# An embedding tower on one core: lookups and pair products taken in turns on TensorE

## The chip, the cores and the metric

The kernel runs on one core of one Trainium2 chip. The metric is the device time of one execution in microseconds (us); the kernel before has a median of 606.28 us in three runs (603.73 to 606.65). Engines are named as in the profile: PE is TensorE (PEld its weight loads), DVE is VectorE, ACT is ScalarE, POOL is GpSimd, SP is SyncE.

## The reference

For 2048 samples, 27 table rows of 128 numbers each are looked up, all pairs of the 27 are multiplied, and the 351 products go with a dense input through three layers.

```python
e = jnp.stack([tbl_f[ids[:, f]] for f in range(27)], axis=1)        # 2048 x 27 x 128
interactions = jnp.einsum('bfd,bgd->bfg', e, e)
x = interactions.reshape(B, F * F)[:, TRIL_IDX]                      # 351 pairs
z = jnp.concatenate([bottom_mlp_out, x], axis=1)
h = jnp.concatenate([z, bottom_mlp_out], axis=1)
h = jnp.maximum(h @ W_top1 + b_top1, 0.0)                            # 512
h = jnp.maximum(h @ W_top2 + b_top2, 0.0)                            # 256
y = h @ W_top3                                                       # 2048 x 1
```

Tables have 1000 to 125000 rows. Everything is float32.

## The kernel before

The 2048 samples are cut into 16 halves of 128 (h = 0 to 15). Features come in two ways.

Nine small tables ("hot", k = 0 to 8) are kept in SBUF as `parts` (a high and a low part, f32r). They are looked up by matmul: VectorE makes masks (`mask[...] = (hot_i == rowid)`, 1 where a sample's id is the row), and PE multiplies chunks of 125 table rows with a mask. One lookup serves a window of four halves (512 columns), and each half does the share of one part of the window: a **pair** of tables (8 chunks, in each chunk 2 tables x 2 parts = 4 matmuls, 32 in all; in the profile 32 records), and in h = 0, 4, 8, 12 a **single** table besides (10 chunks, 20 matmuls). `AFTER[h]` names them, `look_up` is PE's side, `make_masks` and `copy_lookup` those of VectorE and ScalarE. There are 8 mask buffers; a mask of the next lookup is made when a chunk of the present one has retired (`masks_used`). The copies go to `eH` and ScalarE places them in `eT` (`place_early`, `place_late`).

The other 18 tables are gathered by POOL, 18 indirect DMAs a half (L284), into `rows[:, h % 2]`. PE transposes them (L664, 18 matmuls in five groups) into PSUM banks, VectorE and ScalarE copy them to `eT`. The gathers for h + 2 may start when PE has transposed the rows of h; POOL waits for it group by group (L280 to L288).

The products of a half, the "gram", are 64 matmuls of 58 x 52 columns (L681), two records each in the profile since they are fp32, so 128 records. They go in 4 sets of 32 records over three PSUM banks (`gram_bank`): a set is copied by VectorE (strip 0, L582) and ScalarE (strip 1, L424) into `pairs`, and the fourth set needs the bank of the first. When all four are copied, SP moves `pairs` to `x` (L322). Every two halves form a tile of 256 samples for the layers (`layer1` L700 and L704, `layer2` L736, `layer3` L744), which PE takes in pieces after the gram and between the transposes.

Each engine's stream is written out by hand; semaphores order them against each other. In the loop over h = 1 to 14, PE takes: transposes (with pieces of the layers between), the pair's lookup, the whole gram, the single lookup, layers. VectorE takes: copies of transposes, all masks it may make, the lookup's copy, then the gram's copies (`copy_pairs`). For h = 0 the gram comes first and the pair's lookup after it.

## Time and profile before

| | |
|---|---|
| median of three runs | 606.28 us (603.73 to 606.65) |
| the profiled execution | 607.63 us, its span 605.8 us |
| mean granted clock of PE | 0.806 |
| PE busy | 415.0 us (69%), 3512 matmul records |
| PEld busy | 347.6 us (57%) |
| POOL busy | 300.4 us (50%) |
| DVE busy | 216.8 us (36%) |
| ACT busy | 150.6 us (25%) |
| chain that ended last | PE 57%, "issue" 27%, ACT 4%, DVE 2%, DMA 2% |

The table is from the profile's first page. A busy share is an average over the span. "issue" is time in which an engine waited for nothing that the profile shows. The start of a PE record is when it was begun, but its end is modelled, so when PE's work was really done is read from the engines that waited for it.

### The profile page before, as it was taken

The numbers are of one execution on the slowest core, as the hardware profiler recorded it, in microseconds if no ns is written. First come the engines' busy times: TensorE is split into PE (matmuls) and PEld (weight loads), VectorE is DVE, ScalarE is ACT, GpSimd is POOL, SyncE is SP. The second block draws the span as 40 slices with busy tenths as digits, with TensorE's granted clock in tenths as the row PEclk, the third lists the DMA queues.
The fourth block names the chain that finished last, engine by engine and source line by source line (L and its number), as shares of the span: only waits on it lengthen the run. The fifth ranks groups of instructions, "written<-read, shape, count | busy, mean of one in ns | idle before, by whom it ended". The sixth has DMA issues, their size and how long they took to land.

```text
span 605.8 us, 8753 instructions
## 1 busy us (share of the span) xinstructions
PE 415.0 (69%) x3512; PEld 347.6 (57%) x3512; DVE 216.8 (36%) x396; ACT 150.6 (25%) x333; POOL 300.4 (50%) x295
## 2 busy tenths in 40 slices
PE   2941586874876739768494857959586573946997
PEld 2941475663765638556383736837475562835886
DVE  4842448424251334514223245423313232312230
ACT  3320232030422113121130503213031311403533
POOL 6777623757273741737447271574717364271000
PEclk9966688877895959959597887968779695966999
DMA  8764203112121311113121130212102131120000
GB/s 222 211 202 113 56 23 109 50 49 90 27 79 36 112 35 53 49 34 93 36 75 48 37 107 24 66 51 81 48 30 72 28 94 36 32 52 22 27 8 14
DMA packets 20450, 39.81 MB, mean 66 GB/s; under 512 B 7167, under 2 KB 11475, under 8 KB 20410
## 3 DMA queue, kind: packets, MB, share of 16 engines
q0 software_dynamic: 9312, 18.94, 12.1%
q1 hardware_dynamic: 11036, 20.25, 11.6%
q8 instruction: 28, 0.46, 0.3%
q14 instruction: 12, 0.10, 0.1%
q10 hardware_dynamic: 62, 0.06, 0.0%
HBM read 36.14 MB, written 0.01 MB: 60 GB/s over the span
## 4 chain that ended last, share of the span: by engine, by line
PE 57%; issue 27%; another core or an unknown queue 6%; ACT 4%; DVE 2%; DMA 2%; SPq 1%; ACTq 0%; DVEq 0%
PE gram_bank L681 20%; PE col_bank L650 20%; PE mlp_bank L704 5%; PE mlp_bank L736 5%; PE col_bank L664 2%; PE mlp_bank L700 2%; DMA pairs<-in_tbl 2%; DVE mask L547 1%; ACT eT L389 1%; PE mlp_bank L744 1%; ACT h L440 1%; DVE eT L572 1%; ACT eT L394 1%; ACT parts L372 1%
## 5 line engine op out<-in xcount | busy, mean ns | idle before, releaser
L284 POOL DMA_INDIRECT rows<-in_tbl,idx x288 | 298.6, 1037 | 249.2 <-PE col_bank L664 160.1
L681 PE MATMUL gram_bank<-eT 128*58 128x52 f32 x2048 | 123.4, 261 | 136.7 <-issue 135.2
L681 PEld LDWEIGHTS gram_bank<-eT 128*58 128x58 f32 x2048 | 102.6, 174 | 160.2 <-issue 160.0
L650 PE MATMUL col_bank<-mask,parts 125*128 125x512 f32 (+3 forms) x708 | 157.8, 386 | 18.3 <-DVE mask L547 11.7
L650 PEld LDWEIGHTS col_bank<-mask,parts 125*128 125x128 f32 x708 | 131.7, 209 | 40.5 <-DVE parts L588 11.7
L547 DVE TENSOR_SCALAR mask<-hot_i,rowid 125x1024 fp32r<-125x1024 int32 (+3 forms) x152 | 103.2, 679 | 117.3 <-remote 62.3
L582 DVE COPY pairs<-gram_bank 26x208 f32<-26x208 f32 x128 | 46.7, 365 | 120.0 <-remote 100.0
L424 ACT ACTIVATE pairs<-gram_bank 26x208 f32<-26x208 f32 x128 | 44.0, 344 | 139.8 <-remote 114.1
L381 ACT ACTIVATE eH<-col_bank 128x512 f32<-128x512 f32 (+3 forms) x26 | 13.0, 506 | 226.0 <-remote 150.9
L664 PE MATMUL col_bank<-ident,rows 128*128 128x128 f32 x288 | 41.0, 287 | 31.6 <-ACT eH L381 18.9
L664 PEld LDWEIGHTS col_bank<-ident,rows 128*128 128x128 f32 x288 | 34.8, 148 | 38.1 <-issue 35.6
L572 DVE COPY eT<-col_bank 128x512 f32<-128x512 f32 (+1 forms) x38 | 24.4, 653 | 88.8 <-PE col_bank L664 75.2
L704 PE MATMUL mlp_bank<-x,w 126*128 126x256 f32 (+3 forms) x192 | 44.8, 369 | 0.0
L394 ACT ACTIVATE eT<-eH 128x256 f32<-128x256 f32 (+1 forms) x64 | 36.5, 703 | 10.2 <-DVE eH L564 9.8
L704 PEld LDWEIGHTS mlp_bank<-x,w 126*128 126x128 f32 (+1 forms) x192 | 35.4, 193 | 4.9
L389 ACT ACTIVATE eT<-col_bank 128x512 f32<-128x512 f32 (+1 forms) x42 | 26.0, 629 | 35.2 <-PE col_bank L664 21.0
L736 PE MATMUL mlp_bank<-h,w 128*128 128x256 f32 (+1 forms) x128 | 31.1, 400 | 0.2 <-ACT h L433 0.2
L551 DVE TENSOR_SCALAR mask<-hot_i,rowid 125x512 fp32r<-125x512 int32 (+2 forms) x50 | 20.2, 451 | 25.3 <-DMA hot_i<-in_hot_ids 11.0
L736 PEld LDWEIGHTS mlp_bank<-h,w 128*128 128x128 f32 x128 | 24.7, 208 | 4.2 <-ACT h L433 0.4
L292 POOL DMA_DIRECT2D x<-pairs x3 | 1.6, 533 | 41.2 <-DVE pairs L582 41.2
L700 PE MATMUL mlp_bank<-bottom,w 128*128 128x256 f32 (+1 forms) x64 | 19.8, 391 | 1.2 <-ACT y L449 1.2
L588 DVE TENSOR_TENSOR parts<-pairs,parts 125x1024 fp32r<-125x1024 f32 (+1 forms) x9 | 11.1, 1261 | 14.0 <-ACT parts L372 7.7
(31 smaller groups left out, 82.0 us busy)
## 6 DMA issues: line engine op xcount, KB each, us to landing
hot_i<-in_hot_ids SPq DMA_DIRECT2D x13, 512.0 KB
rows<-in_tbl,idx POOLq DMA_INDIRECT x288
pairs<-in_tbl SPq DMA_DIRECT2D x8, 448.0 KB
hot_i<-in_hot_ids SPq DMA_DIRECT2D x5, 256.0 KB
bottom<-in_bottom SPq DMA_DIRECT2D x8, 128.0 KB
hot_i<-in_hot_ids SPq DMA_DIRECT2D x2, 384.0 KB
x<-pairs SPq DMA_DIRECT2D x16, 39.0 KB
pairs<-in_tbl SPq DMA_DIRECT2D x1, 560.0 KB
```

Of the source, the lines that this page charges most:

```text
L284: pool.indirect_dma_start(out=rows_of(h, g)[:, i * D:(i + 1) * D], out_offset=None, in_=tables[GATHERED_TABLES[f]], in_offset=bass.Indirec ...
L389: nc.scalar.activation(out, src, ACT.Copy).then_inc(col_copied[fill % BANKS], 1)
L394: return nc.scalar.activation(eT[:, :, first:last].rearrange("p s f -> p f s"), eH[:, first:last, at:at + HALF], ACT.Copy)
L424: last = nc.scalar.activation(pairs_of(s, 1, j), gram_of(n % BANKS, 1, j), ACT.Copy)
L547: last = nc.vector.tensor_scalar(mask[0:ROWS, entry % MASKS, 0:2 * size], ids, row_of(ks[0], c), None, ALU.is_equal)
L582: last = nc.vector.tensor_copy(pairs_of(s, 0, j), gram_of(n % BANKS, 0, j))
L650: last = nc.tensor.matmul(col_bank[fill % BANKS][:, 0:size], parts[k][0:ROWS, part, c * D:(c + 1) * D], mask[0:ROWS, entry % MASKS, at:at ...
L664: last = nc.tensor.transpose(col_bank[fill % BANKS][:, i * HALF:(i + 1) * HALF], rows_of(h, g)[:, i * D:(i + 1) * D], ident[:, :])
L681: last = nc.tensor.matmul(gram_bank[n % BANKS][COLUMNS * t:COLUMNS * t + GRAM_ROWS, q, 0:PACK * (F - 1)], eT[:, a:a + PACK, :].rearrange(" ...
L700: nc.tensor.matmul(layer1_out(u, m), w1[:, X_CHUNKS, m * 128:(m + 1) * 128], bottom[:, buf, at:at + size], start=True, stop=False)
L704: last = nc.tensor.matmul(layer1_out(u, m).rearrange("p (h s) -> p h s", s=HALF), w1[0:k, c, m * 128:(m + 1) * 128], x[0:k, buf, at // HAL ...
L736: last = nc.tensor.matmul(layer2_out(u, m), w2[:, c, m * 128:(m + 1) * 128], h1[:, c, at:at + size], start=(c == 0), stop=(c == N1 // 128 ...
```

## The change

On PE, `look_up_and_multiply` takes a half's pair of lookups in eight turns: one chunk (4 matmuls), then half a gram set (8 matmuls, 16 records). The wait for the features to be placed (`features_placed`) stands after the first chunk. This holds for h = 0 to 14, h = 0 too, where the gram had come first. The single lookup and the last half stay as they were. On VectorE, `masks_and_pairs` makes two of the eight masks ahead of each set's copy, and copies the lookup after the four sets; before, all masks and the lookup's copy came ahead of the four. On ScalarE the gram's copies now come ahead of the lookup's copy.

```diff
@@ ScalarE, the loop over h @@
+                copy_pairs(h)
                 if h < LAST:
                     copy_lookup(AFTER[h][0])
-                copy_pairs(h)
-                if h < LAST:
                     place_early(h + 1)
@@ VectorE @@
+            def masks_and_pairs(h):
+                single = AFTER[h][1:]
+                ahead = AFTER[h + 1][:1] if h + 1 < LAST else []
+                early = ENTRIES[single[0]] if single else 0
+                each = MASKS // SETS
                 for s in range(SETS):
+                    for entry in range(s * each, (s + 1) * each):
+                        if entry < early:
+                            make_masks(single[0], slice(entry, entry + 1))
+                        elif ahead:
+                            make_masks(ahead[0], slice(entry - early, entry - early + 1))
+                    copy_set(h, s)
+                copy_lookup(AFTER[h][0])
+                if early and ahead:
+                    make_masks(ahead[0], slice(MASKS - early, MASKS))
+                for n in single:
+                    copy_lookup(n)
...
@@ PE @@
+            def look_up_and_multiply(n, h):
+                parts_of_set = TURNS // SETS
+                chunks, steps = CHUNKS[LOOKUPS[n][0][0]] // TURNS, STRIP // PACK // parts_of_set
+                for turn in range(TURNS):
+                    look_up(n, slice(turn * chunks, (turn + 1) * chunks))
+                    if turn == 0:
+                        features_placed(h)
+                    at = turn % parts_of_set * steps
+                    multiply_set(h, turn // parts_of_set, slice(at, at + steps))
...
-            multiply_pairs(0)
-            for n in AFTER[0]:
+            look_up_and_multiply(AFTER[0][0], 0)
+            for n in AFTER[0][1:]:
                 look_up(n)
...
-                look_up(AFTER[h][0])
-                multiply_pairs(h)
+                look_up_and_multiply(AFTER[h][0], h)
                 for n in AFTER[h][1:]:
                     look_up(n)
```

On PE in a half like h = 2, before: the last transposes (L664), the pair's lookup (L650), the gram (L681), `layer1` (L700, L704).

```order
L664 MATMUL col_bank<-ident,rows 128x128 x18
L650 MATMUL col_bank<-mask,parts 128x512 x32
L681 MATMUL gram_bank<-eT 58x52 x64
L700 MATMUL mlp_bank<-bottom,w 128x256
L704 MATMUL mlp_bank<-x,w 128x256 x3
```

The same place on PE after the change (L665 transposes, L651 lookup, L683 gram); the pattern of two rows goes on until there are eight of each.

```order
L665 MATMUL col_bank<-ident,rows 128x128 x18
L651 MATMUL col_bank<-mask,parts 128x512 x4
L683 MATMUL gram_bank<-eT 58x52 x8
L651 MATMUL col_bank<-mask,parts 128x512 x4
L683 MATMUL gram_bank<-eT 58x52 x8
L651 MATMUL col_bank<-mask,parts 128x512 x4
L683 MATMUL gram_bank<-eT 58x52 x8
```

The 32 lookup matmuls and 64 gram matmuls stand in eight alternating groups of 4 and 8; their numbers are the same.

On VectorE in a half like h = 6, before: copies of transposes (L572), masks (L547), the lookup's copy (L564), the gram's copies (L582).

```order
L572 COPY eT<-col_bank 128x128x4
L572 COPY eT<-col_bank 128x128x3
L547 TENSOR_SCALAR mask<-hot_i,rowid 125x1024 x8
L564 COPY eH<-col_bank 128x512
L582 COPY pairs<-gram_bank 26x26x8 x8
```

And after the change (L573, L548, L582, L565).

```order
L573 COPY eT<-col_bank 128x128x4
L573 COPY eT<-col_bank 128x128x3
L548 TENSOR_SCALAR mask<-hot_i,rowid 125x1024 x2
L582 COPY pairs<-gram_bank 26x26x8 x2
L548 TENSOR_SCALAR mask<-hot_i,rowid 125x1024 x2
L582 COPY pairs<-gram_bank 26x26x8 x2
L548 TENSOR_SCALAR mask<-hot_i,rowid 125x1024 x2
L582 COPY pairs<-gram_bank 26x26x8 x2
L548 TENSOR_SCALAR mask<-hot_i,rowid 125x1024 x2
L582 COPY pairs<-gram_bank 26x26x8 x2
L565 COPY eH<-col_bank 128x512
```

Each set's two copies now stand behind two masks, and the lookup's copy behind the last set.

## Rows read from the trace of the kernel before

**Rows 1.** The page's groups: busy, mean ns of one | idle before, its releaser

```profile
L284 POOL DMA_INDIRECT rows<-in_tbl,idx x288 | 298.6, 1037 | 249.2 <-PE col_bank L664 160.1
L681 PE MATMUL gram_bank<-eT 128*58 128x52 f32 x2048 | 123.4, 261 | 136.7 <-issue 135.2
```

**Rows 2.** Timeline, h = 6, PE: start us, us, engine, line, records [idle before]

```profile
276.07 7.54 PE L650 MATMUL col_bank<-mask,parts 125*128 125x512 f32 x32 [0.37 <-issue]
283.54 0.79 PE L681 MATMUL gram_bank<-eT 128*58 128x52 f32 x21
284.65 0.32 PE L681 MATMUL gram_bank<-eT 128*58 128x52 f32 x4 [0.33 <-issue]
...
298.92 4.24 PE L681 MATMUL gram_bank<-eT 128*58 128x52 f32 x78 [0.46 <-issue]
```

**Rows 3.** Timeline, POOL: first and last of 18 gathers, and the next first

```profile
273.21 0.94 POOL L284 DMA_INDIRECT rows<-in_tbl,idx  x1 [9.45 <-PE col_bank L664]
...
295.71 0.94 POOL L284 DMA_INDIRECT rows<-in_tbl,idx  x1 [0.30 <-issue]
309.62 0.94 POOL L284 DMA_INDIRECT rows<-in_tbl,idx  x1 [12.97 <-PE col_bank L664]
```

**Rows 4.** Timeline, h = 6, VectorE: masks, the lookup's copy, the gram's copies

```profile
279.46 3.30 DVE L547 TENSOR_SCALAR mask<-hot_i,rowid 125x1024 fp32r<-125x1024 int32 x4 [3.50 <-DMA hot_i<-in_hot_ids]
283.25 0.85 DVE L547 TENSOR_SCALAR mask<-hot_i,rowid 125x1024 fp32r<-125x1024 int32 x1 [0.48 <-PE col_bank L650]
284.69 0.75 DVE L547 TENSOR_SCALAR mask<-hot_i,rowid 125x1024 fp32r<-125x1024 int32 x1 [0.59 <-remote]
...
287.59 0.75 DVE L547 TENSOR_SCALAR mask<-hot_i,rowid 125x1024 fp32r<-125x1024 int32 x1 [0.69 <-issue]
288.50 0.69 DVE L564 COPY eH<-col_bank 128x512 f32<-128x512 f32 x1 [0.16 <-issue]
299.13 1.61 DVE L582 COPY pairs<-gram_bank 26x208 f32<-26x208 f32 x4 [9.93 <-remote]
```

**Rows 5.** Timeline, PE: the last gram burst of h = 2, 3, 4, 9

```profile
154.83 3.48 PE L681 MATMUL gram_bank<-eT 128*58 128x52 f32 x83 [0.28 <-issue]
...
190.52 2.23 PE L681 MATMUL gram_bank<-eT 128*58 128x52 f32 x38 [0.47 <-issue]
...
223.69 5.34 PE L681 MATMUL gram_bank<-eT 128*58 128x52 f32 x105 [0.46 <-issue]
...
410.13 0.67 PE L681 MATMUL gram_bank<-eT 128*58 128x52 f32 x9 [0.98 <-issue]
```

**Rows 6.** DMA queues, SP's packets, 198.1 to 222.6 (h = 4), 383.8 to 410.3

```profile
q1 hardware_dynamic: 529, 1.00, 14.3%
...
q1 hardware_dynamic: 8, 0.01, 0.1%
```

**Rows 7.** Timeline: two masks of h = 1, each after a chunk; gram in h = 9

```profile
107.32 0.75 DVE L547 TENSOR_SCALAR mask<-hot_i,rowid 125x1024 fp32r<-125x1024 int32 x1 [2.39 <-PE col_bank L650]
108.96 0.76 DVE L547 TENSOR_SCALAR mask<-hot_i,rowid 125x1024 fp32r<-125x1024 int32 x1 [0.88 <-PE col_bank L650]
...
394.62 2.33 PE L681 MATMUL gram_bank<-eT 128*58 128x52 f32 x79
```

**Rows 8.** Timeline, h = 0, PE: the gram, then lookups of the pair and the single

```profile
79.50 1.40 PE L681 MATMUL gram_bank<-eT 128*58 128x52 f32 x45 [1.54 <-ACT eT L394]
...
85.94 12.09 PE L650 MATMUL col_bank<-mask,parts 125*128 125x512 f32 x52
```

**Rows 9.** Windows: length, PE, PEld, DVE, ACT, POOL busy (x), PEclk, DMA share, GB/s

```profile
298.90:303.00 4.10, 4.08 (x78) 4.07 (x78) 2.19 (x6) 2.04 (x6) 0.00 (x0) 0.50 0.00 0
...
303.10:309.00 5.90, 5.90 (x28) 5.13 (x28) 0.73 (x2) 3.64 (x8) 0.00 (x0) 0.94 0.09 24
...
281.00:286.80 5.80, 3.96 (x40) 3.04 (x39) 3.83 (x6) 0.00 (x0) 4.58 (x5) 1.00 0.17 45
286.80:298.90 12.10, 3.38 (x22) 2.27 (x21) 1.55 (x3) 0.60 (x1) 7.72 (x8) 0.50 0.20 50
```

More of the change, by code:

```diff
@@ L31 @@
 SLOTS = 2
+TURNS = 8
 STAGES = 3
@@ L478, in _ @@
             copy_pairs(0)
+            copy_lookup(AFTER[0][0])
             place_early(1)
-            for n in AFTER[0]:
+            for n in AFTER[0][1:]:
                 copy_lookup(n)
@@ L594, in _ @@
                 make_masks(n)
[L596 to L601 removed]
+            make_masks(AFTER[0][0])
+            masks_and_pairs(0)
             dve.wait_ge(weights_loaded, 16 * WEIGHT_LOADS)
             nc.vector.tensor_tensor(w1[:, X_CHUNKS, :], w1[:, X_CHUNKS, :], wb, ALU.add).then_inc(w1_summed, 1)
[L604 to L607 removed]
             for h in range(1, HALVES):
@@ L610, in _ @@
                     copy_transposed(h, g)
-                if h == LAST:
-                    copy_pairs(h)
-                elif len(AFTER[h]) == 2:
-                    pair, single = AFTER[h]
-                    make_masks(single)
-                    make_masks(AFTER[h + 1][0], slice(0, free))
-                    copy_lookup(pair)
-                    copy_pairs(h)
-                    make_masks(AFTER[h + 1][0], slice(free, MASKS))
-                    copy_lookup(single)
-                else:
-                    if h + 1 < LAST:
-                        make_masks(AFTER[h + 1][0])
-                    copy_lookup(AFTER[h][0])
-                    copy_pairs(h)
+                if h < LAST:
+                    masks_and_pairs(h)
+                else:
+                    for s in range(SETS):
+                        copy_set(h, s)
         @block.tensor
@@ L632, in fill_free, with look_up @@
                     pe.wait_ge(col_copied[fill % BANKS], fill // BANKS)
-            def look_up(n):
+            def look_up(n, part=slice(None)):
                 ks, _, wide = LOOKUPS[n]
                 size, chunks = wide * HALF, CHUNKS[ks[0]]
-                for k in ks:
+                for k in ks if range(chunks)[part][0] == 0 else ():
                     fill_free(lookup_fill(n, k))
@@ L641, in look_up @@
                         pe.wait_ge(low_made, k + 1)
-                for c in range(chunks):
+                for c in range(chunks)[part]:
                     entry = entries_to(n) + c * len(ks) // 2
@@ L755, in _ @@
             pe.wait_ge(pads_cleared, 1)
-            multiply_pairs(0)
-            for n in AFTER[0]:
+            look_up_and_multiply(AFTER[0][0], 0)
+            for n in AFTER[0][1:]:
                 look_up(n)
@@ L785, in _ @@
             transpose(LAST, 4)
-            multiply_pairs(LAST)
+            features_placed(LAST)
+            for s in range(SETS):
+                multiply_set(LAST, s)
             layer3(TILES - 2)
```

50 lines of the change are left out of this document (21 added, 29 removed).

## Prediction

> **What bounds the kernel now.** Three views, in this order. First the page's groups: 288 gathers on POOL and 2048 gram matmul records on PE; before the gram records PE stands idle for 136.7 us, all but 1.5 us of it charged to "issue", that is to nothing the profile can name [rows 1]. Second, PE's timeline of one half, h = 6 [rows 2]: the pair of lookups is recorded smoothly, 32 records in 7.54 us, then 21 gram records in a burst, then three or four at a time with gaps, until at 298.92 the remaining 78 go through in 4.24 us. Third, who else moves then. POOL issues its 18 gathers from 273.21 to 296.65 [rows 3], and PE is free again 2.3 us after the last one. The next 18 start at 309.62, after the gram, the MLP and the next transposes, because POOL waits for PE's transposes. So a half is a loop: gathers (some 23.5 us), 2.3 us, then what PE still has to do, then transposes, then gathers again. Only what PE does **after the gathers** lies on the path; what it does beside them is free.
>
> How fast PE really is beside the gathers is read from its waiters, since ends of matmuls are modelled. VectorE makes a mask each time a chunk (4 lookup records) retires: one wait ends at 284.69, the next but one at 287.59, so 1.45 us a chunk or 0.36 us a record, where they were recorded at 0.236 us [rows 2, 4]. The first gram set (32 records) retires when VectorE copies it at 299.13: (299.13 - 287.59) / 32 = 0.36 us a record again [rows 4]. A record with 512 columns and one with 52 cost the same. Beside the gathers PE therefore seems limited by the **number of instructions**, not by their work. In PE's timeline the records run some 32 ahead of what has retired (the first set was recorded complete at about 288).
>
> How many of a half's 160 records (32 lookups, 128 gram) are out when PE is freed differs: the last burst has 83, 38, 105 and 9 gram records in h = 2, 3, 4 and 9 [rows 5]. Over h = 2 to 12, h = 4, 8, 12 are like the 105, four like the 83, three like the 38, one like the 9; h = 1 is like the 38 and h = 13 like the 105 with lookups half as wide. The half with 105 had 529 packets of SP's queue beside its gathers, the one with 9 had 8 [rows 6], which again looks like a shared allowance of events.
>
> **The change, part by part.** The number of instructions on PE is the same. What moves is their order: 8 turns of 4 lookup records and 16 gram records instead of 32 and then 128. If the allowance counts instructions, a half gets as many records past the gathers as before, but what is **left over** is no longer all gram: a fifth of it is lookups.
>
> Prices. At full clock a lookup record takes 0.236 us [rows 2] and a gram record 0.031 (45 in 1.40 us [rows 8]); a turn 4 x 0.236 + 16 x 0.031 = 1.44 us. At half clock a chunk takes 108.96 - 107.32 = 1.64 us, 0.41 a record [rows 7], and a gram record 4.24 / 78 = 0.054 [rows 2]; a turn 2.5 us. The clock is 0.50 from 286.8 to 303 and 0.94 after it [rows 9], so I take the first 4.5 us after the gathers at half clock (1.8 turns), the rest at full.
> - Like 105: 55 records past, 5.25 turns left: 4.5 + 3.45 x 1.44 = 9.5 us for 5.3 now [rows 5]: +4.2, three times 12.6; h = 13 about +2.
> - Like 83 or 78: 3.9 to 4.15 turns left: 7.5 to 7.9 us for 4.2 and 3.5: +3.9, four times 15.6.
> - Like 38: 1.9 turns left: 4.6 for 2.2: +2.4, four times 9.6.
> - Like 9: 0.45 turn: +0.4.
>
> Together **+40 us**, if the same count gets past. That is one end. The other end: in the stretch before PE slows down, PE is limited by its work (a chunk of 8 instructions in 0.94 us), and a turn of 40 instructions in 1.44 us would get 19 more a us through, if slowing sets in by the clock on the wall and not by a count. In h = 6 that stretch is some 4 us (the first mask that waits late is at 283.25, before it the chunks were in time): 1.9 turns gained. In the halves like 105 I take 2 us (1 turn), in those like 38 the whole lookup. Gained: 3 x 1.4 for the first kind, 4 x 2.8, 4 x 4.6, 1.1 and 1.4: **-36 us**. Nothing in the trace settles which end holds. For a count: in h = 9 PE was never slowed in the lookups and then slowed right after 79 gram records in 2.33 us [rows 7]. For the clock on the wall: at 79 records the count was far higher than in h = 6. I take half, -18.
>
> Front, h = 0: the gram waits for ScalarE until 79.50 and runs to 85.94, 6.4 us for 128 records that take 4.0 at full clock, then the pair of lookups [rows 8]. Interleaved, the first chunk can go under that wait and most turns run at full clock: -2 us, between 0 and -4.
>
> VectorE: two masks now stand ahead of each set's copy. Behind them on VectorE wait the copy, and behind that PE's fourth set (turn 7), which needs the first set's bank. The masks wait for SP's transfer of ids; in h = 6 the first four start at 279.46 and take 3.30 us [rows 4]. Two masks then end by 281.1, the copy by 281.9, and PE reaches turn 7 at 276.07 + 6 x 1.44 = 284.7 at the earliest. Nothing, with 2.8 us to spare; without that cover it would cost what the ids are late. The sets' copies by VectorE and ScalarE now fall beside the gathers, but the last set's does not, and a copy from a lookup's bank comes after it on each (VectorE's takes 0.69 us [rows 4]): under the 5 to 6 us of MLP that PE runs next, so nothing, except in h = 1, which has no MLP there (at most 1.5 us). The new wait for the last features stands after the first chunk instead of after eight; they are copied within half a us of its start, under 0.94 us of chunk. POOL and SP keep their order; nothing is moved past their queues.
>
> Sum: 607.63 (the profiled execution; its span is 605.8, 1.8 us lie around it) + 40 - 18 - 2 = 627.6. That execution is 1.35 us above the median of the runs, so **626 us** on the median's scale.
>
> A rule that speaks for the change: the clock follows how densely PE works, and PE falls to 0.50 in the thin gram phase at 286.8 [rows 9]. The Trainium skill, "TensorE: Matmul & The Clock Gate", section "HAM oscillation — how this bites in real kernels", has it that gaps in PE's work throw it back to the low clock, so that work placed into the gaps should hold it up. By it this case would come out as the third rival below; the rows so far only show that the clock held while slowed lookups ran (281 to 286.8, 1.00) and fell in thin gram.
>
> **The rivals.**
> 1. A pure count. +40 - 2: 644; with all leftover turns at half clock (5.25 x 2.5 for 9.5, and so on, +60) 664. For it: 0.36 us a record for both kinds. Against it: the counts in h = 6 and 9 differ threefold.
> 2. Slowing by the clock on the wall. 607.6 + 40 - 36 - 2 - 1.35 = 608. For it: POOL's pace is constant.
> 3. The clock stays up. All leftover turns at 1.44 us: +2.3, +1.7, +0.5 for the three kinds, +17 in all with h = 13, less half of what is gained before slowing (14) and the front's 2: 608. Against it: at 0.36 us a record a turn of 1.44 us of work takes 7.2 us.
> 4. The other side: the gaps belong to runs of gram matmuls. "Issue" stands ahead of gram and hardly ahead of lookups [rows 1, 2]; four lookups between would cover the gaps, PE would be done with its 160 records (11.6 us) long before the gathers end, and the last bursts (44 us over h = 1 to 13, from 5.34 down to 0.67 [rows 5]) would leave the path: 563. It decides if a chunk of lookups beside gathers retires at its own pace; in h = 6 it did not [rows 4].
> That the change does not do what it says is excluded by the order: PE's stream is in program order.
>
> **How the numbers follow.** Chances: my forecast (612 to 640) 0.35, pure count 0.17, by the wall 0.13, clock up 0.12, gaps covered 0.18, other losses 0.05 (VectorE's copies late after all). A measurement of this kernel tells about 0.5% from no change, 603.2 to 609.3: of the wall and clock cases 0.14 lie in it and 0.05 below. So faster 0.23, same 0.14, slower 0.63. The range takes in the wall case and the pure count with part of its cold end, and leaves out the covered gaps and the far end: 599 to 650.
>
> **What would show it.** In the profile after, PE's timeline of a half should show thin records of both lines beside the gathers, a last burst that holds lookups, longer than 4.2 us (7 us in halves like h = 6), and gathers that start some 2 us later in each period. A half whose gram is over before the gathers end, or a period near 25 us, would prove rival 4. If the waits charged to "issue" keep their sum but the burst is short, the wall case holds. A granted clock of 1.00 beside the gathers would be rival 3.

## The result, and the profile after

The changed kernel takes **677.51 us** (median of 4 runs, 675.77 to 679.25) where the kernel before, timed beside it, takes 606.25 (603.73 to 606.65): ratio 1.1185, 95% interval 1.1143 to 1.1228. A later pair of timings gave 675.94 against 603.92, ratio 1.1199 (1.1134 to 1.1263). The prediction said slower, 626 us, at most 650. The direction was right, and so was the place, the work after the gathers; the loss is 71 us instead of 20.

The profiled execution has a span of 675.2 us, 69.4 more than before. The page's groups of the changed kernel, as [rows 1]:

```profile
L285 POOL DMA_INDIRECT rows<-in_tbl,idx x288 | 283.6, 985 | 329.0 <-PE col_bank L665 238.9
L651 PE MATMUL col_bank<-mask,parts 125*128 125x512 f32 (+3 forms) x708 | 216.4, 441 | 47.1 <-issue 27.4
L683 PE MATMUL gram_bank<-eT 128*58 128x52 f32 x2048 | 127.3, 242 | 144.5 <-issue 144.0
```

Gram matmuls are as busy as before (127 against 123 us) and idle time charged to "issue" now stands ahead of the lookups too. A gather is shorter (985 ns instead of 1037), but POOL waits 239 us for PE's transposes instead of 160: the whole loss and more in one number, 79 us, of which shorter gathers give a part back. PE's timeline of h = 6, as [rows 2] (start us, length, line, records, idle before):

```profile
296.36 1.17 PE L651 MATMUL col_bank<-mask,parts 125*128 125x512 f32 x4 [0.37 <-issue]
297.45 0.64 PE L683 MATMUL gram_bank<-eT 128*58 128x52 f32 x16
...
316.57 0.32 PE L683 MATMUL gram_bank<-eT 128*58 128x52 f32 x1 [1.17 <-issue]
317.96 2.62 PE L651 MATMUL col_bank<-mask,parts 125*128 125x512 f32 x4 [1.06 <-issue]
320.51 1.04 PE L683 MATMUL gram_bank<-eT 128*58 128x52 f32 x16
321.48 2.08 PE L651 MATMUL col_bank<-mask,parts 125*128 125x512 f32 x4
323.49 1.04 PE L683 MATMUL gram_bank<-eT 128*58 128x52 f32 x16
324.46 1.39 PE L651 MATMUL col_bank<-mask,parts 125*128 125x512 f32 x4
325.78 0.64 PE L683 MATMUL gram_bank<-eT 128*58 128x52 f32 x16
326.35 1.19 PE L651 MATMUL col_bank<-mask,parts 125*128 125x512 f32 x4
...
329.74 0.48 PE L714 MATMUL mlp_bank<-bottom,w 128*128 128x256 f32 x1
```

The last of this half's 18 gathers ends at 316.35. Two turns get past in a burst, then PE is thin (20 records from 301.0 to 317.2, windows below; the third turn among them), and behind the gathers stand **five** turns of lookups and gram, 11.8 us, where the kernel before had 78 gram records in 4.24 us [rows 2]. The last burst holds lookups, as predicted. A turn takes 3.5 and 3.0 us first, then 1.9 and 1.7. VectorE in the same half, as [rows 4]:

```profile
301.37 0.75 DVE L548 TENSOR_SCALAR mask<-hot_i,rowid 125x1024 fp32r<-125x1024 int32 x1 [5.12 <-issue]
311.04 0.75 DVE L548 TENSOR_SCALAR mask<-hot_i,rowid 125x1024 fp32r<-125x1024 int32 x1 [8.91 <-remote]
319.51 0.74 DVE L582 COPY pairs<-gram_bank 26x208 f32<-26x208 f32 x2 [7.72 <-remote]
```

Two masks stand beside the gathers, where there were eight at 279.46 to 288.34 [rows 4]: the other six now wait behind the first set's copy, and that waits for the thin gram. The windows, as [rows 9] (length, busy time and count of PE, PEld, DVE, ACT, POOL, granted clock, DMA share, GB/s):

```profile
301.00:317.20 16.20, 4.81 (x20) 2.64 (x20) 1.51 (x2) 0.00 (x0) 12.00 (x12) 0.61 0.21 54
...
318.00:323.40 5.40, 5.17 (x24) 2.79 (x23) 2.87 (x6) 1.38 (x4) 0.00 (x0) 0.50 0.01 3
323.40:330.00 6.60, 6.60 (x78) 4.88 (x78) 3.64 (x6) 0.85 (x3) 0.00 (x0) 0.89 0.00 0
```

**The account.** Cut both traces at the ends of the gathers, h = 1 to 13, and the 69.4 us come out in five parts. "Past" is how many of a half's pair lookups and gram matmuls (160 records) have their start by 1.9 us after the last gather, mean of h = 2 to 12; "work after" is from the last gather's end to the start of the last of these 160, summed over h = 1 to 13 (negative where all 160 start before the gathers end); "rest" is from there to the next gather, and "tail" what follows the last of h = 13. The other rows are experiments told below.

| | past | start of h = 1 | gathers | work after | rest | tail | span |
|---|---|---|---|---|---|---|---|
| before | 92 | 98.7 | 307.2 | 70.5 | 79.9 | 49.4 | 605.8 |
| changed | 64 | 93.6 | 292.7 | 163.0 | 74.6 | 51.3 | 675.2 |
| PE's order undone | 65 | 92.4 | 295.0 | 95.9 | 74.9 | 49.8 | 608.0 |
| before, masks twice | 116 | 99.5 | 320.2 | 40.6 | 85.3 | 49.5 | 595.1 |
| before, ScalarE busy | 99 | 98.4 | 308.3 | 69.3 | 86.0 | 50.4 | 612.4 |

The loss is 92.5 us of work after the gathers and 2.0 in the tail; shorter gathers (-14.6), the rest (-5.3) and the front (-5.2) give 25 back.

### The profile page after: what moved, and what is told of

Read it like the earlier page. It is cut to its first block, busy times and chain, and to the rows that moved or that the text cites. A ratio compares the mean times of both kernels' runs of the same rounds, so it can differ in the third digit from the quotient of the medians.

```text
span 675.2 us, 8846 instructions
## 1 busy us (share of the span) xinstructions
PE 459.6 (68%) x3512; PEld 344.8 (51%) x3512; DVE 215.0 (32%) x396; ACT 150.6 (22%) x333; POOL 285.4 (42%) x295
## 4 chain that ended last, share of the span: by engine, by line
PE 59%; issue 28%; another core or an unknown queue 5%; ACT 3%; DVE 2%; DMA 1%; SPq 0%; ACTq 0%; DVEq 0%
PE col_bank L651 27%; PE gram_bank L683 18%; PE mlp_bank L718 4%; PE mlp_bank L750 4%; PE col_bank L665 2%; PE mlp_bank L714 2%; DVE mask L548 1%; DMA pairs<-in_tbl 1%; PE mlp_bank L758 1%; ACT eT L390 1%; ACT h L441 1%; ACT parts L373 1%; DVE eT L573 1%; ACTq L512 0%
## 5 line engine op out<-in xcount | busy, mean ns | idle before, releaser
L285 POOL DMA_INDIRECT rows<-in_tbl,idx x288 | 283.6, 985 | 329.0 <-PE col_bank L665 238.9
L651 PE MATMUL col_bank<-mask,parts 125*128 125x512 f32 (+3 forms) x708 | 216.4, 441 | 47.1 <-issue 27.4
L683 PE MATMUL gram_bank<-eT 128*58 128x52 f32 x2048 | 127.3, 242 | 144.5 <-issue 144.0
L683 PEld LDWEIGHTS gram_bank<-eT 128*58 128x58 f32 x2048 | 96.1, 151 | 202.8 <-issue 201.2
L651 PEld LDWEIGHTS col_bank<-mask,parts 125*128 125x128 f32 x708 | 139.5, 231 | 82.6 <-issue 45.7
L548 DVE TENSOR_SCALAR mask<-hot_i,rowid 125x1024 fp32r<-125x1024 int32 (+3 forms) x152 | 103.1, 678 | 188.5 <-remote 100.9
L582 DVE COPY pairs<-gram_bank 26x208 f32<-26x208 f32 x128 | 46.7, 365 | 108.3 <-remote 93.7
L665 PE MATMUL col_bank<-ident,rows 128*128 128x128 f32 x288 | 40.5, 283 | 19.8 <-ACT eH L382 10.9
L573 DVE COPY eT<-col_bank 128x512 f32<-128x512 f32 (+1 forms) x38 | 24.4, 652 | 75.3 <-PE col_bank L665 57.6
L665 PEld LDWEIGHTS col_bank<-ident,rows 128*128 128x128 f32 x288 | 34.0, 145 | 26.9 <-issue 24.4
L750 PE MATMUL mlp_bank<-h,w 128*128 128x256 f32 (+1 forms) x128 | 28.1, 372 | 0.2 <-ACT h L434 0.2
L750 PEld LDWEIGHTS mlp_bank<-h,w 128*128 128x128 f32 x128 | 22.6, 190 | 3.3 <-ACT h L434 0.4
L382 ACT ACTIVATE eH<-col_bank 128x512 f32<-128x512 f32 (+3 forms) x26 | 12.9, 506 | 48.4 <-remote 36.2
L607 DVE TENSOR_TENSOR parts<-pairs,parts 125x1024 fp32r<-125x1024 f32 (+1 forms) x9 | 11.0, 1253 | 12.9 <-ACT parts L373 7.8
```

What stands on the lines that cost most here:

```text
L285: pool.indirect_dma_start(out=rows_of(h, g)[:, i * D:(i + 1) * D], out_offset=None, in_=tables[GATHERED_TABLES[f]], in_offset=bass.Indirec ...
L548: last = nc.vector.tensor_scalar(mask[0:ROWS, entry % MASKS, 0:2 * size], ids, row_of(ks[0], c), None, ALU.is_equal)
L582: last = nc.vector.tensor_copy(pairs_of(s, 0, j), gram_of(n % BANKS, 0, j))
L651: last = nc.tensor.matmul(col_bank[fill % BANKS][:, 0:size], parts[k][0:ROWS, part, c * D:(c + 1) * D], mask[0:ROWS, entry % MASKS, at:at ...
L665: last = nc.tensor.transpose(col_bank[fill % BANKS][:, i * HALF:(i + 1) * HALF], rows_of(h, g)[:, i * D:(i + 1) * D], ident[:, :])
L683: last = nc.tensor.matmul(gram_bank[n % BANKS][COLUMNS * t:COLUMNS * t + GRAM_ROWS, q, 0:PACK * (F - 1)], eT[:, a:a + PACK, :].rearrange(" ...
```

## The experiments

The theories, as the expectations name them. **A**: beside the gathers PE gets a limited number of instructions through whatever they weigh, and what is left over is on the path. **S** (against it): alternating wide and narrow matmuls is dear in itself. **V**: copies queued behind masks on VectorE are the cost. **D**, formed after the result: mask making on VectorE beside the gathers is what lets PE run unslowed for part of them, and the change moved it away. All ratios are against runs of the kernel before on the same chip, timed beside it. Some expectations speak of 82 records past in the kernel before; that is the count of h = 6 alone, and the mean, counted as in the table, is 92.

**PE's order undone, VectorE's and ScalarE's kept** (against the changed kernel, also in h = 0):

```
-                look_up_and_multiply(AFTER[h][0], h)
+                look_up(AFTER[h][0])
+                features_placed(h)
+                for s in range(SETS):
+                    multiply_set(h, s)
```

> The changed kernel with TensorE's part undone alone: the pair's 32 lookups, then the whole gram; VectorE and ScalarE keep the changed order (masks between the sets' copies, the lookup's copy last). Theory A (beside the gathers TensorE gets a number of instructions through, whatever their work, and interleaving leaves lookups for after the gathers): all of the loss is in TensorE's order, so this is back at 600 to 612 us. Rival V (VectorE's copies queued behind masks hold up TensorE's fourth set): stays at 660 to 680 us.

609.88 us, ratio 1.007 (1.003 to 1.011). PE's timeline of h = 6:

```profile
275.57 7.52 PE L651 MATMUL col_bank<-mask,parts 125*128 125x512 f32 x32 [1.24 <-issue]
...
296.14 4.07 PE L683 MATMUL gram_bank<-eT 128*58 128x52 f32 x81 [0.47 <-issue]
```

This splits the loss. The records past are as few as in the changed kernel (65), so **the new order on VectorE and ScalarE, without PE's, takes 27 records** from them (this kernel keeps both, so it doesn't tell the two apart; the experiments on masks below point to VectorE). Its price, +25.4 us of work after, is paid back by gathers shorter by 12.3, a rest shorter by 5.0 and a front shorter by 6.3. **PE's alternation alone costs 67 us**, all of it work after (95.9 to 163.0) at the same count. V is out: its copies stand behind the same masks here.

**The gram whole, ahead of the pair's lookups** (VectorE's copies ahead of its masks to fit):

```
-                look_up_and_multiply(AFTER[h][0], h)
+                features_placed(h)
+                for s in range(SETS):
+                    multiply_set(h, s)
+                look_up(AFTER[h][0])
```

> The changed kernel with the gram of a half taken whole and ahead of the pair's lookups, no alternation; VectorE copies the four sets first and makes the masks after. Theory A: what gets past beside the gathers (some 60 records) is all gram, all 32 lookups are left for after, so as slow as the interleaved one or slower, 675 to 705 us. Rival S (alternating between the two kinds of matmul is what costs): no alternation, so 600 to 615 us.

684.96 us (one run). PE, h = 6:

```profile
306.77 1.40 PE L684 MATMUL gram_bank<-eT 128*58 128x52 f32 x45 [0.79 <-DVE eT L573]
...
328.86 2.94 PE L684 MATMUL gram_bank<-eT 128*58 128x52 f32 x53 [0.35 <-issue]
331.72 8.45 PE L652 MATMUL col_bank<-mask,parts 125*128 125x512 f32 x32
```

No alternation at all, and no faster than the changed kernel: 68 to 75 gram records get past in h = 2 to 13 (85 in h = 1), and all 32 lookups stand behind the gathers, in h = 6 for 8.45 us. S falls as the account of the whole loss, A holds: what counts is which kind is left over.

**No gathers** beyond h = 1, in both kernels (rows of later halves are left stale, which changes the output):

```
-            for h in range(HALVES):
+            for h in range(2):
```

> The kernel before without the gathers of halves 2 to 15 (their rows are those of halves 0 and 1, so the output is not the reference's). Theory A: the gaps ahead of gram records charged to issue (135 us) vanish, gram sets retire at 1 to 1.6 us each, a half takes 20 to 22 us instead of 35, 430 to 470 us in all. Rival (the gaps belong to runs of small matmuls as such): they stay, over 560 us.

> The changed kernel without the gathers of halves 2 to 15 (their rows are those of halves 0 and 1, so the output is not the reference's). Compared with the kernel before without them: theory A: only the cost of alternating itself is left, a turn takes 1.44 to 1.7 us, so 0 to 25 us slower. Rival S (alternating costs by itself): the whole 70 us slower.

423.79 and 423.89 us, one run each. The gram's group in each page:

```profile
L681 PE MATMUL gram_bank<-eT 128*58 128x52 f32 x2048 | 61.2, 220 | 22.9 <-DVE pairs L582 20.7
```

```profile
L683 PE MATMUL gram_bank<-eT 128*58 128x52 f32 x2048 | 79.8, 221 | 0.7 <-issue 0.7
```

Without gathers the 135 us of "issue" are gone from both. The times are equal, but alternating isn't free. Windows from the first lookup of a half to the last gram record, before and changed, both at clock 1.00 (columns as in [rows 9]):

```profile
228.60:239.50 10.90, 10.89 (x160) 9.33 (x160) 8.64 (x15) 3.21 (x9) 0.00 (x0) 1.00 0.02 5
```

```profile
200.35:213.80 13.45, 13.45 (x160) 9.40 (x160) 7.50 (x14) 2.44 (x7) 0.00 (x0) 1.00 0.17 51
```

The same 160 records take 2.5 us more in eight turns, 0.32 us a turn. In the kernel before every second half has a wait of 2.4 us or more for VectorE's copies (the 20.7 us above), which the alternation takes away (0.7 us of idle time are left), so the two cancel here. A part of S is true then: an estimate of what it costs in the changed kernel, with 4.8 turns left over in a half, is 4.8 x 0.32 us x 13 = 20 of the 67 us. The rest is that some 18 lookups a half are left over where gram records were.

**Plain DMAs by POOL instead of indirect ones**, the same bytes from fixed rows (wrong rows, so another output), in the kernel before:

```
-                        pool.indirect_dma_start(
-                            out=rows_of(h, g)[:, i * D:(i + 1) * D], out_offset=None, in_=tables[...],
-                            in_offset=bass.IndirectOffsetOnAxis(ap=idx[:, h, f:f + 1], axis=0),
+                        pool.dma_start(
+                            rows_of(h, g)[:, i * D:(i + 1) * D], tables[...][h % 7 * HALF:(h % 7 + 1) * HALF, :]
```

> The kernel before with each indirect gather of POOL replaced by a plain DMA from POOL of 128 consecutive rows of the same table (same bytes, same row size of 512 B, same queue; the rows are not those looked up, so the output is not the reference's). If it is the traffic or POOL's queue that slows TensorE: gaps ahead of gram records stay over 100 us and the time near 606 us (580 to 620). If it is what POOL does for an index (reading ids, writing descriptors): gaps under 30 us, and the time below 520 us.

> The kernel before with the rows of halves 2 to 15 loaded by SP's queue as plain DMAs of 128 consecutive rows, POOL idle after half 1 (output is not the reference's). If POOL's way of making DMAs slows TensorE: the gaps vanish, 430 to 520 us. If it is the row traffic itself into SBUF: gaps stay over 100 us, 580 us or more.

414.77 us, and 431.93 with the same transfers issued by SP. The page with POOL's plain DMAs:

```profile
L284 POOL DMA_DIRECT2D rows<-in_tbl x288 | 172.0, 611 | 191.3 <-PE col_bank L663 184.7
L680 PE MATMUL gram_bank<-eT 128*58 128x52 f32 x2048 | 62.4, 222 | 25.9 <-DVE pairs L581 23.4
```

So it is neither the bytes nor POOL's queue, but the **indirect** DMAs that slow PE. It is one run each; the seven runs of the kernel before beside them all took 601 to 608 us, so PE was being slowed on that chip.

**Each lookup matmul halved in columns**, so twice as many (kernel before):

```
+                        for a in (0, cut):
+                            last = nc.tensor.matmul(
+                                col_bank[fill % BANKS][:, a:a + cut], ...,
+                                mask[0:ROWS, entry % MASKS, at + a:at + a + cut], ...
```

> The kernel before with every lookup matmul cut into two of half the columns: same work, twice the lookup instructions. Theory A (a count gets past): of some 80 records that get past a half's gathers 64 are now lookups, some 32 more gram records are left for after them, 1 to 1.7 us a half and more in the halves where under 64 get past (there lookups are left too): 620 to 650 us. Rival W (TensorE is slowed in proportion to work or time, not to instructions): 600 to 612 us.

654.73 us (one run): the same columns in 64 records of 256 instead of 32 of 512 cost 49 us, 5 more than expected at most. Of the 47 us of span, 24.3 are work after the gathers of h = 1 to 13, 1.9 us a half where A said 1 to 1.7. Another 21.3 lie ahead of h = 1, where the halved lookups of the front also pass singly, up to 2.6 us apart, beside the first gathers, and 8.3 in the tail (gathers and rest give 6.8 back); these were not in A's sum. In the main A again: beside the gathers instructions are what is scarce.

**The layers' pieces ahead of the gram** (kernel before; wide work first, narrow work last):

```
                 look_up(AFTER[h][0])
+                if h % 2 == 0 and h >= 2:
+                    layer1(h // 2 - 1, range(4))
+                if h % 2 == 1 and h >= 3:
+                    layer2(h // 2 - 1)
                 multiply_pairs(h)
```

> The kernel before with the pieces of the layers (layer1 and layer2 of an earlier tile) taken between the pair's lookup and the gram, instead of after the gram, and layer1 in one piece. Theory A turned round: instructions with much work belong beside the gathers and the small gram ones after them; 16 to 32 layer records leave the path (0.29 us each) and as many gram records enter it (0.05 us each): 4 to 5 us a half over 13 halves, 545 to 580 us. Rival W: the layers are slowed as much as the gram would have been, 595 to 612 us.

**564.34 us**, ratio 0.9321 (0.9246 to 0.9396): the fastest of the kernels with the right output that ran where PE is slowed. PE in an even half:

```profile
259.00 7.50 PE L647 MATMUL col_bank<-mask,parts 125*128 125x512 f32 x32 [0.37 <-issue]
266.33 0.59 PE L697 MATMUL mlp_bank<-bottom,w 128*128 128x256 f32 x2
...
273.36 0.47 PE L678 MATMUL gram_bank<-eT 128*58 128x52 f32 x6
...
280.67 4.85 PE L678 MATMUL gram_bank<-eT 128*58 128x52 f32 x99 [0.46 <-issue]
```

Layer 1's 32 wide records, 7.0 us from 266.33 to 273.36, are issued beside the gathers in the place of gram records that cost 0.049 us each (4.85 / 99) once the gathers are over. In the table's terms the rest falls from 79.9 to 26.9 us and the work after rises from 70.5 to 83.7. This is the changed kernel's mistake with its sign turned.

**Where PE is not slowed.** The kernels for theory D, and a variant that puts the single lookups first too, ran first on a chip where the kernel before takes 424.09 us (5 runs, 423.28 to 425.67).

> The kernel before with every mask of halves 1 on made twice. Theory D: VectorE is busy 1.6 us of each chunk instead of 0.75, some 6 us longer beside the gathers; TensorE runs freely in that time and more gram records get past: 560 to 598 us. Rival (VectorE has no part in it): 603 to 620 us.

> The changed kernel with every mask of halves 1 on made twice by VectorE (the second writes the same values), 0.75 us of VectorE work more a mask. Theory D (VectorE's mask making holds back POOL's work on its gathers and with it the slowing of TensorE; the change left VectorE idle beside the gathers, which is why fewer records got past): more records past than the 64 of the changed kernel, gathers longer than 22.2 us, 620 to 665 us. Rival: VectorE has no part in it, 675 to 700 us, since its copies come later.

> A control for theory D: the kernel before with ScalarE's copy of each lookup (128x512, 0.60 us) done eight times, some 4 us more of ScalarE work beside the gathers of halves 1 on. Theory D (it is the port that VectorE and POOL share): no gain, 603 to 625 us. Rival (any busy engine beside the gathers frees TensorE): under 598 us.

> The kernel with the layers ahead of the gram, and in halves 4, 8 and 12 (and 0) the single table's 20 lookups ahead of the gram too. Theory A (instructions with much work belong beside the gathers): 20 records of 0.24 us leave the path in three halves and as many gram records enter it, but in these halves only some 60 records got past, so part of them stays: 545 to 563 us. Rival: no change, 562 to 570 us.

484.59 (ratio 1.1435, 1.1329 to 1.154), 463.69 (1.0942, 1.0909 to 1.0974), 435.45 (one run) and 420.92 us (0.9922, 0.9888 to 0.9956). They presuppose a slowed PE and say nothing on D; with doubled masks VectorE bounds the kernel (masks are 31% of the chain that ended last). One trace shows more. Layers and single lookups first, PE and POOL:

```profile
201.39 3.62 PE L678 MATMUL gram_bank<-eT 128*58 128x52 f32 x128
...
202.99 0.94 POOL L284 DMA_INDIRECT rows<-in_tbl,idx  x1 [0.30 <-issue]
```

A whole half's gram goes through in 3.62 us in the middle of indirect gathers, with no gap. So beside the same gathers PE can be slowed or not, and this is not bound to one chip: the results number this one 7, and in the last experiment below the kernel before took 604.48 us on a chip with the same number.

**Theory D, where PE is slowed** (kernel before 603.92 us, 7 runs). Each mask made twice over:

```
-                        last = nc.vector.tensor_scalar(mask[...], ids, row_of(ks[0], c), None, ALU.is_equal)
+                        for i in range(2 if n > FRONT + 1 else 1):
+                            if i > 0:
+                                dve.drain()
+                            last = nc.vector.tensor_scalar(mask[...], ids, row_of(ks[0], c), None, ALU.is_equal)
```

> The kernel before with each mask from half 0 on made twice over (same result, about 12 us more of VectorE a half). Where the kernel before takes about 606 us: theory D (mask making on VectorE holds POOL's gathers back and lets PE run unslowed meanwhile) says that more lookups and gram matmuls get past beside the gathers, 100 to 150 instead of 82 a half, gathers of 24 to 28 us, and a time of 560 to 598 us; if masks do nothing for PE, 606 to 625 us with the counts of before. Where the kernel before takes 424 us: 484 us as already measured, VectorE being the bound.

> Control: the kernel before with each of ScalarE's copies of a transposed column made eight times over, so that ScalarE and not VectorE has more work beside the gathers. Where the kernel before takes about 606 us: theory D says no gain, 603 to 625 us; if any engine's work beside the gathers frees PE, or any delay that spreads the gathers out, 560 to 598 us. Where the kernel before takes 424 us: 435 us as already measured.

> The changed kernel with each mask from half 0 on made twice over. Where the kernel before takes about 606 us: theory D says 620 to 665 us, less than the 677 of the changed kernel, for VectorE then has work beside the gathers again; if masks do nothing for PE, 677 to 700 us. Where the kernel before takes 424 us: 464 us as already measured.

> The changed kernel once more, unaltered, beside the kernel before on one chip. If the kernel before takes about 606 us there: 670 to 682 us. If it takes about 424 us there (PE isn't slowed beside the gathers): theory A says that the change costs nothing of its own, since the two kernels without gathers took 423.8 and 423.9 us, so a ratio of 0.99 to 1.01; a theory by which alternating lookups and gram matmuls is dear in itself says 1.03 or more.

Masks twice in the kernel before: 593.81 us (2 runs), ratio 0.9843 (0.9749 to 0.9938): **more work on VectorE makes the kernel faster**, if only by some 1.6%. Past rises from 92 to 116, work after falls from 70.5 to 40.6 us, and gathers get 12.9 us longer. ScalarE's copies eight times over: 611.28, ratio 1.0133 (1.0039 to 1.0226), past 99, work after 69.3; this work of ScalarE brings no gain. (What was made eight times are the copies out of a lookup's bank, and not, as the expectation has it, those of transposed columns. In h = 5 they start 7.1 us after the first lookup and take 5.3 us, so the control has neither the place nor the length of the doubled masks.) VectorE, PE and POOL in h = 5 with doubled masks:

```profile
243.02 13.35 DVE L550 TENSOR_SCALAR mask<-hot_i,rowid 125x1024 fp32r<-125x1024 int32 x16 [0.98 <-PE col_bank L653]
...
241.75 7.54 PE L653 MATMUL col_bank<-mask,parts 125*128 125x512 f32 x32 [0.30 <-DVE eT L575]
249.21 1.81 PE L684 MATMUL gram_bank<-eT 128*58 128x52 f32 x49
251.39 1.41 PE L684 MATMUL gram_bank<-eT 128*58 128x52 f32 x35 [0.37 <-issue]
...
246.71 1.38 POOL L284 DMA_INDIRECT rows<-in_tbl,idx  x1 [0.30 <-issue]
...
256.80 0.95 POOL L284 DMA_INDIRECT rows<-in_tbl,idx  x1 [0.30 <-issue]
```

```profile
243.00:256.40 13.40, 9.90 (x124) 7.92 (x122) 12.06 (x16) 2.71 (x7) 10.96 (x9) 0.98 0.16 40
```

While 16 masks of 1024 columns run back to back, POOL's gathers take 1.38 us instead of 0.95 and PE gets 124 records through in 13.4 us at clock 0.98; a stretch as long from just behind the first lookup of h = 6 of the changed kernel (297.6 to 311.0) has 51 records at clock 0.75, most of them in the first burst. All 160 are out before the gathers end, in h = 3, 5, 7 and 9 alike. The masks' lengthening of POOL's gathers agrees with the Trainium skill, "SBUF — State Buffer", section "SBUF: two separate sides", by which some VectorE operations lock the port pair that GpSimd needs to write its DMAs' descriptors. The skill counts this as a loss, and here the kernel got faster with it.

An early start helps but is no condition. In h = 3, 5, 7 and 9 the first mask starts 1.3 to 2.0 us after the first lookup. In h = 2, 6 and 10 it starts 7.5, 6.3 and 4.8 us after it, and 130, 110 and 160 records get past, where the kernel before has 80, 82 and 114: PE is slowed at first and speeds up while the masks run. In h = 11, with doubled masks of 768 columns, 78 get past instead of 74. In h = 4, 8 and 12, where the single lookup's masks come first and were not doubled, it is 55, 43 and 59 instead of 54, 67 and 61. Masks and gathers of h = 6, h = 10 and h = 11:

```profile
275.20 4.94 DVE L550 TENSOR_SCALAR mask<-hot_i,rowid 125x1024 fp32r<-125x1024 int32 x6 [6.43 <-issue]
...
277.20 1.38 POOL L284 DMA_INDIRECT rows<-in_tbl,idx  x1 [0.30 <-issue]
...
413.29 13.34 DVE L550 TENSOR_SCALAR mask<-hot_i,rowid 125x1024 fp32r<-125x1024 int32 x16 [4.47 <-PE col_bank L653]
...
445.64 7.70 DVE L550 TENSOR_SCALAR mask<-hot_i,rowid 125x768 fp32r<-125x768 int32 x11 [1.38 <-PE col_bank L653]
...
448.80 1.11 POOL L284 DMA_INDIRECT rows<-in_tbl,idx  x1 [0.30 <-issue]
```

It would be wrong to read a rule on the masks' width from this. In the kernel with the busy ScalarE, whose masks are as before, h = 11 has 149 records past (74 in the kernel before), with single masks of 768 columns and gathers of 1.5 us. Its PE and POOL:

```profile
460.05 7.54 PE L654 MATMUL col_bank<-mask,parts 125*128 125x512 f32 x32 [0.37 <-issue]
467.52 2.23 PE L685 MATMUL gram_bank<-eT 128*58 128x52 f32 x75
...
465.05 1.50 POOL L284 DMA_INDIRECT rows<-in_tbl,idx  x1 [0.31 <-issue]
```

Nor can the halves of the kernel before decide it. Past is 122, 123, 151 and 114 in h = 3, 5, 9 and 10, whose masks follow each other nearly unbroken, 82 and 80 in h = 6 and 7, where most come one at a time, and 54, 67 and 61 in h = 4, 8 and 12, whose masks are mostly narrow. But each mask waits until PE is done with a chunk, so unbroken masks can as well be the result of a PE that keeps its pace: in h = 7 they come 1.4 us apart and more though the first starts 1.7 us after the first lookup. Only the kernels in which the masks themselves were moved or doubled speak for a cause.

The changed kernel with doubled masks: 673.97 us (2 runs), 2 us below the 675.94 of the changed kernel beside it and within its runs, past 64 as before. D had promised 620 to 665. The reason is in its order: only the first two entries' masks are made beside the gathers (2.8 us of mask time a half instead of 1.4), the others still wait behind the first set's copy. So this was not the test I took it for.

**Comparisons at the place itself.** 36 comparisons of 256 columns into unused room, made by VectorE in each half as soon as its transposed columns are copied (changed kernel), and 7 + 18 of them in the kernel with the layers first:

```
+            def make_spare(count):
+                for i in range(count):
+                    nc.vector.tensor_scalar(y[64:64 + 61, :].bitcast(f32r), idx[64:64 + 61, :, :]...[:, 0:TILE],
+                                            rowid[64:64 + 61, 0:1], None, ALU.is_equal)
+                    dve.drain()
```

> The changed kernel, in which VectorE, once a half's transposed columns are copied and before its masks, makes 36 comparisons of the mask's kind (61x256, int32 from SBUF to SBUF, into room that nothing reads), about 12 us of work beside the gathers. Where the kernel before takes about 606 us: theory D says that more lookups and gram matmuls get past, 95 or more records of all kinds a half beside the gathers instead of 80, gathers of 24 to 26 us instead of 22.5, and 610 to 660 us; if the masks' time beside the gathers isn't what frees PE, 677 to 690 us and 80 records. Where the kernel before takes 424 us: 424 to 450 us.

> The kernel before with the layers' pieces between the pair's lookup and the gram (564 us before), and 7 such comparisons behind the transposed columns' copies and 18 ahead of the pairs' copies in each half, about 9 us of VectorE's idle time beside the gathers. Where the kernel before takes about 606 us: theory D says 535 to 560 us, with over 110 records a half beside the gathers instead of 95; if it is not so, 564 to 575 us, since the copies of the gram sets come a little later. Where the kernel before takes 424 us: 420 to 440 us.

718.52 us (2 runs; kernel before 604.48), ratio 1.189 (1.1814 to 1.1965), and 630.42 (3 runs), ratio 1.0377 (1.028 to 1.0473), both far off what D said. VectorE, PE and POOL of the first, h = 7:

```profile
347.88 16.25 DVE L532 TENSOR_SCALAR y<-idx,rowid 61x256 fp32r<-61x256 int32 x36
...
361.43 0.32 PE L692 MATMUL gram_bank<-eT 128*58 128x52 f32 x1 [1.10 <-issue]
...
352.08 1.06 POOL L285 DMA_INDIRECT rows<-in_tbl,idx  x1 [0.31 <-issue]
```

They start 0.3 us after the first lookup and run unbroken, but hold POOL back little (1.06 us), and PE gets **fewer** records past, 52 instead of 64. The time after the gathers did not grow (162.0 us); of the 39 us over the changed kernel's span, 12.9 are longer gathers and 27 lie in the tail, where in two more halves the comparisons stand ahead of the masks and copies. The second kernel is no test of D: much of its added work came after the gathers. In h = 4 the last gather ends at 223.50, and then VectorE and PE run

```profile
233.10 6.83 DVE L528 TENSOR_SCALAR y<-idx,rowid 61x256 fp32r<-61x256 int32 x16 [0.22 <-issue]
...
240.86 1.84 PE L688 MATMUL gram_bank<-eT 128*58 128x52 f32 x32 [5.40 <-DVE pairs L587]
```

so the last gram set waits 5.4 us for copies that stand behind the comparisons; work after rises from 83.7 us (layers first) to 132.6. The first kernel says that D in the form "VectorE's work between SBUF places frees PE" is wrong. What stands is narrower: doubling the masks of 1024 columns let more records past in every half of h = 2 to 10 that has them, and 36 close comparisons of 61x256, which hold a gather to 1.06 us only, did not. That it is the hold on the gathers that matters, to 1.4 or 1.5 us, is a guess that fits these traces.

## Why the prediction was right in sign and wrong in size

Against the kernel before, the sum of the prediction was +40 for lookups left over, -18 given back, -2 in front: +20 us. The spans show +92.5, nothing, and -5.2, with -14.6 in gathers, -5.3 in the rest and +2.0 in the tail: +69.4.

- **What bounds the kernel** held. Work beside the gathers is nearly free, work after them is on the path, and both kinds of record weigh nearly the same beside them: shown by the gram-first kernel (on average 73 gram records of a half get past alone, against 65 of both kinds with PE's order undone), by halved lookups, and by runs without gathers.
- **"The leftovers contain lookups: +40"** was the right mechanism, and its size, about 3 us a half, is where most of the miss lies: 92.5 us in place of 40. PE's alternation alone cost 67 us. Two terms were short. *The price of a turn*: I took 2.5 us at half clock and 1.44 at full. In h = 6 the cold turns took 3.5 and 3.0 us and the warm ones 1.9 and 1.7 (timeline above). The kernel without gathers has the same warm pace at clock 1.00: there four lookups take 1.13 us and not 4 x 0.236, and the 16 gram records behind them 0.57 and not 16 x 0.031. A price for the change from one kind to the other was not in the sum. A cold lookup was priced from two masks [rows 7] at 0.41 us; 2.62 / 4 and 2.08 / 4 are 0.65 and 0.52. *The number of turns*: with 64 records past, 4.8 turns are left on average, not the 3.9 and 1.9 taken for the middle kinds.
- **"If the same count gets past"** was the failed assumption, and with it **VectorE's order at nothing**. I looked for who waits for the delayed masks, found nobody, and as to the time that part was right: with PE's order undone the kernel takes 609.9. What I did not ask is what the masks did to others while they ran. Past fell from 92 to 65 with the order on VectorE and ScalarE. Without PE's it is repaid by shorter gathers and fronts; under alternation each of the 27 records becomes part of a turn with lookups in it.
- **The give-back of 18 us** (slowing by the clock on the wall) did not exist, and the rows could have told. It rests on a stretch of "some 4 us" of h = 6 in which PE keeps its pace, since the masks before 283.25 were in time. But the first four of them had waited for the ids [rows 4] and say nothing of PE. The others wait for chunks 5 to 8. Those of chunks 5, 6 and 8 start at 283.25, 284.69 and 287.59, that is 7.18, 8.62 and 11.52 us after the first lookup at 276.07 [rows 2, 4]: for 20, 24 and 32 records 0.36 us each, from the first one on. In h = 6 there was no stretch to gain from. The threefold counts of h = 9 I took for a second theory and halved the sum between both; why single halves differ so in the kernel before stays open. The changed kernel shows counts of 55 to 79 in h = 2 to 13, near a pure count. That is **rival 1**, with a lower count than I gave it; its cold end, 664, was the nearest number I wrote, and I gave the whole rival 0.17.
- **Front -2** was -5.2, and not for the reason given: with PE's order undone it is -6.3, so it isn't the interleaving that gains there. Gathers shorter by 14.6 us were not in the sum at all: [rows 3] shows 0.94 us gathers, while the page's mean was 1037 ns [rows 1]; the long ones stand beside masks.
- **Rivals 3 and 4** fell as the rows had spoken: clock 0.61 beside the gathers and 0.50 right after, no gap covered. The rule that I cited for rival 3 (the Trainium skill, "TensorE: Matmul & The Clock Gate", "HAM oscillation — how this bites in real kernels") found no use where PE gets one record in 0.8 us (20 in 16.2), so that no work could be placed in the gaps; in the doubled-masks kernel, where records did get through, the clock was 0.98.
- The **range** ended at 650 because I took the same-count assumption into both of its ends. A bound for "VectorE with few wide masks beside the gathers" was missing though the trace had halves for it: h = 4, 8 and 12, with 54 to 67 records past.

**Open.** Why indirect DMAs of POOL slow PE, why only in some sets of runs, why the count past differs so from half to half with the same order, and whether it is the hold on POOL itself that keeps PE at its pace: no run held POOL back by another means. VectorE's part and ScalarE's in the loss of 27 records were not separated. Masks of 1024 columns placed beside the gathers in the changed kernel were not tried.

## What to carry to other kernels

Where an engine gets through a limited number of instructions in a stretch whatever they weigh, give it the heaviest instructions for that stretch and leave the lightest for behind it: moving layer pieces ahead of the gram gained 42 us, moving gram ahead of lookups lost 80. Before an engine's work is moved "at no cost" because nobody waits for it, look at what its neighbours did while it ran, half by half: a row that is faster beside it is part of the price. When counts of one pattern differ between repeats, find what differs in those stretches before averaging over two theories, and mind which of two things that go together waits for the other. And two kernels that take the same time can hide a cost in one of them: alternating cost 2.5 us a half under cover of a wait.

## What the runs showed of the hardware

- Beside POOL's **indirect** DMAs (18 in some 22.5 us) PE got 64 lookup and gram records a half through in the changed kernel and 92 in the kernel before, while plain DMAs of the same bytes from the same queue left it unhindered: 606 against 415 us for the kernel before.
- The same kernel takes **606 or 424 us** in all its runs timed together, even on a chip with the same number. Where it takes 424, PE is not slowed beside the gathers, and the time is that of the kernel without gathers (423.8). Only kernels timed side by side can be compared.
- Masks of 1024 columns (int32 to fp32r in SBUF), made back to back, lengthen a gather from 0.94 to 1.38 us, of 768 columns to 1.11, comparisons of 61x256 to 1.06. Single masks of 768 columns 0.9 us apart went with 1.50 to 1.52. Doubling those of 1024 columns raised the records past from 92 to 116 a half.
- Alternating 4 lookups of 512 columns with 16 gram records (8 matmuls) takes 1.13 us for the 4 and 0.57 for the 16 at clock 1.00, against 0.93 and 0.45 from long runs at the same clock (7.47 / 32 and 3.62 / 128 a record).
